# Embedding lookups, pairwise products and a small MLP on one core: a looped program against an unrolled one with a gather ring

## The reference, cut to what matters

```python
e = jnp.stack([tbl_0[ids[:, 0]], ..., tbl_25[ids[:, 25]]], axis=1)
combined = jnp.concatenate([dense_features[:, None, :], e], axis=1)
interactions = jnp.einsum('bfd,bgd->bfg', combined, combined)
z = jnp.concatenate([dense_features, interactions[:, _TRIU_I, _TRIU_J]], axis=1)
h = jnp.concatenate([z, r_dense_features], axis=1)      # 607 columns
h = jnp.maximum(h @ W_top1 + b_top1, 0.0)               # 512
h = jnp.maximum(h @ W_top2 + b_top2, 0.0)               # 256
y = h @ W_top3                                          # 1
```

## Time and profile before

| | |
|---|---|
| device time, median of 3 | 491.5 us (488.62 to 497.02) |
| profiled execution: span | 791.1 us |
| TensorE matmuls busy | 487.2 us, 3016 records |
| VectorE busy | 226.9 us |
| ScalarE busy | 262.0 us |
| GpSimd busy | 305.1 us, of it 304.3 us in 320 gathers |
| mean granted TensorE clock | 0.756 of full speed |

### The profile page before, as it was taken

The page is one execution under the profiler, slowest core; times in us unless marked ns, Lnnn a source line. Parts: engine busy times, 40 slices in busy tenths (PEclk is TensorE's granted clock), DMA queues, the critical chain, the costliest instruction groups (busy, mean ns, idle before and its releaser), DMA issues.

```text
span 791.1 us, 8476 instructions
## 1 busy us (share of the span) xinstructions
PE 487.2 (62%) x3016; PEld 424.6 (54%) x3016; DVE 226.9 (29%) x296; ACT 262.0 (33%) x632; POOL 305.1 (39%) x327
## 2 busy tenths in 40 slices
PE   6407566526748086580956719476393855939977
PEld 4306556426637085470855518464282745827866
DVE  3207251222313142321413213133131332313231
ACT  1115131512416033160522615025150432405762
POOL 6751707370442606336072541705327071350000
PEclk8757767666959679596886959768596866958997
DMA  5620202110110101111010110101101020010000
GB/s 128 198 72 11 54 7 55 28 52 9 34 37 19 53 1 45 27 24 46 0 50 20 35 35 9 52 10 40 30 17 50 3 53 17 27 43 1 1 1 0
DMA packets 20003, 27.57 MB, mean 35 GB/s; under 512 B 10940, under 2 KB 13508, under 8 KB 19985
## 3 DMA queue, kind: packets, MB, share of 16 engines
q0 software_dynamic: 10240, 20.99, 10.3%
q1 hardware_dynamic: 9728, 6.32, 2.9%
q10 hardware_dynamic: 16, 0.01, 0.0%
HBM read 27.29 MB, written 0.01 MB: 35 GB/s over the span
## 4 chain that ended last, share of the span: by engine, by line
PE 42%; another core or an unknown queue 22%; issue 20%; ACT 12%; DVE 3%; DMA 0%; ACTq 0%; SPq 0%; DVEq 0%
PE gram L415 16%; PE ring L453 12%; PE ring L372 11%; ACT xt L585 6%; ACT pairs_or_h L606 4%; DVE onehot L705 2%; PE idb L361 1%; PE ring L442 1%; PE ring L476 1%; ACT xt L574 1%; ACT A L592 1%; DMA pairs_t_or_h<-in_ids 0%; DVE A L786 0%; DVE x_or_h_split L772 0%
## 5 line engine op out<-in xcount | busy, mean ns | idle before, releaser
L321 POOL DMA_INDIRECT rows<-in_tbl,ids_tile x320 | 304.3, 951 | 401.6 <-PE ring L400 306.7
L415 PE MATMUL gram<-xt 128*128 128x104 f32 x1024 | 161.4, 318 | 31.6 <-issue 28.3
L415 PEld LDWEIGHTS gram<-xt 128*128 128x128 f32 x1024 | 153.1, 233 | 38.5 <-issue 33.6
L372 PE MATMUL ring<-onehot,table_hi 125*128 125x256 f32 x368 | 113.1, 334 | 37.6 <-DVE onehot L705 31.3
L705 DVE TENSOR_TENSOR onehot<-idb,vrow 125x2048 fp32r<-125x2048 f32 x48 | 110.0, 2292 | 59.8 <-remote 47.2
L453 PE MATMUL ring<-x_or_h_split,w_hi 128*128 128x256 f32 (+1 forms) x384 | 95.6, 322 | 47.9 <-issue 40.2
L785 DVE COPY A<-gram 32x208 f32<-32x208 f32 x64 | 32.2, 503 | 309.6 <-remote 171.3
L591 ACT COPY A<-gram 32x208 f32<-32x208 f32 x64 | 32.4, 506 | 244.4 <-remote 163.9
L453 PEld LDWEIGHTS ring<-x_or_h_split,w_hi 128*128 128x128 f32 (+1 forms) x384 | 74.1, 219 | 64.0 <-issue 56.8
L372 PEld LDWEIGHTS ring<-onehot,table_hi 125*128 125x128 f32 x368 | 79.9, 217 | 48.0 <-issue 40.2
L372 PE MATMUL ring<-onehot,table_lo 125*128 125x256 f32 x368 | 103.7, 308 | 1.4 <-issue 1.4
(11 more groups left out here) (46 smaller groups left out, 272.9 us busy)
## 6 DMA issues: line engine op xcount, KB each, us to landing
rows<-in_tbl,ids_tile POOLq DMA_INDIRECT x320
xt<-in_tbl SPq DMA_DIRECT2D x6, 500.0 KB
rows<-in_r_dense_features SPq DMA_DIRECT2D x16, 64.0 KB
A<-in_W_top SPq DMA_DIRECT2D x2, 256.0 KB
xt<-in_W_top SPq DMA_DIRECT2D x2, 256.0 KB
pairs_or_h<-in_W_top SPq DMA_DIRECT2D x1, 512.0 KB
ids_tile<-in_ids SPq DMA_DIRECT2D x16, 13.0 KB
pairs_t_or_h<-in_ids SPq DMA_DIRECT2D x1, 208.0 KB
```

Source lines behind the costliest of these rows:

```text
L321: pool.indirect_dma_start(rows[:, t % 2, 1 + r, :], None, aps[f"tbl_{f}"], bass.IndirectOffsetOnAxis(ap=ids_tile[:, t, f:f + 1].bitcast(U3 ...
L372: last = pe.matmul(ps[:, 0:HALF], part[:, m, k, :], onehot[:, buf, k, :], start=(k == 0 and part is table_hi), stop=(k == KT - 1 and part ...
L415: last = pe.matmul(gram[:, s % 2, g // PER_BANK, col:col + QUAD * NA], four, cols, start=True, stop=True)
```

## The change

- The hardware loop is gone; `stages()` yields every stage of four rounds of 512 samples, and all waits are on constants.
- Eight tables instead of six are looked up by one-hot (15 and 19 are added), so 18 are gathered: 288 gathers instead of 320.
- A lookup covers 512 samples, 16 matmuls of 512 columns; its one-hot comes in four quarters (`CH = 4`) of 125 x 1024 through three slots. The ids are spread by a DMA that broadcasts a row of the transposed ids (`spread_ids` on SyncE) and a ScalarE copy into PSUM.
- `rows` is a ring of 45 single rows, not two places of a tile. A gather waits for the transposes of what lay in its slot, and **the first of each six gathers waits until all six of the group ahead have landed**.
- Layers 1 and 2 are plain float32 matmuls of 256 columns, 4 for each block of 128 outputs, without upper and lower parts of weights and activations.
- Of each product step VectorE copies three blocks, ScalarE one; half of the picking of pairs for the first half of a round goes to VectorE.
- All ids are loaded at once, and the eight table loads are split into 112 and 13 partitions. The rows of W_top1 are put in another order on the host so that the one-hot features come last.

```diff
-LOOKUP_TABLES = [2, 5, 10, 12, 13, 14]
+LOOKUP_TABLES = [2, 5, 10, 12, 13, 14, 15, 19]
+ROWS = 45
+GROUP = 6
...
         def _(pool):
-            def gathers(r, t):
-                pool.wait_ge(ids_slot[t], 16 * (r + t // 2 + 1))
-                pool.sem_inc(tiles_begun, 1)
-                for r, f in enumerate(GATHER_TABLES):
-                    pool.indirect_dma_start(
-                        rows[:, t % 2, 1 + r, :], None, aps[f"tbl_{f}"],
-                        bass.IndirectOffsetOnAxis(ap=ids_tile[:, t, f:f + 1].bitcast(U32), axis=0),
-                    ).then_inc(rows_landed[t % 2], 16)
+            def gathers(k):
+                for g, f in enumerate(GATHER_TABLES):
+                    i = k * NG + g
+                    if i >= ROWS and (g == 0 or group_of(i - ROWS) != group_of(i - ROWS - 1)):
+                        pool.wait_ge(ring_filled, filled("rows", *group_of(i - ROWS)))
+                    if i and i % GROUP == 0:
+                        q, u = divmod(i // GROUP - 1, NG // GROUP)
+                        pool.wait_ge(rows_landed[q % 3][u], 16 * GROUP * (q // 3 + 1))
+                    pool.indirect_dma_start(
+                        rows[:, i % ROWS, :], None, aps[f"tbl_{f}"],
+                        bass.IndirectOffsetOnAxis(ap=ids_all[:, k, f:f + 1].bitcast(U32), axis=0),
+                    ).then_inc(rows_landed[k % 3][g // GROUP], 16)
...
         def _(pe):
+                for c in range(CH):
+                    pe.wait_ge(onehot_ready, CH * u + c + 1)
+                    for k in range(KC):
+                        for part in (table_hi, table_lo):
+                            last = pe.matmul(ps, part[:, m, c * KC + k, :], onehot[:, (CH * u + c) % SLOTS, k, :],
...
-                terms = [(k, rows, wp, xp) for k, rows in blocks for wp, xp in ((0, 0), (1, 0), (0, 1))]
+                pe.matmul(ps, w1[:, 0, n * P:(n + 1) * P], x_dense[:, h, :], start=True, stop=False)
+                for k, (k0, w) in enumerate(K_PAIR):
+                    last = pe.matmul(ps, w1[0:w, 1 + k, n * P:(n + 1) * P], x[0:w, k, :], start=False, stop=(k == KX - 1))
...
         def _(dve):
                 dve.tensor_copy(*product_views(t, s, 0))
+                dve.tensor_copy(*product_views(t, s, 1))
+                dve.tensor_copy(*product_views(t, s, 2)).then_inc(gram_dve, 1)
```

More of the change, by code:

```diff
@@ L137, in ring_start @@
[L137 to L157, removed]
+    WARM_UP = 16
@@ L186, in build @@
         b2 = sb("b2", [P, H2 // P])
[L188 to L193, removed]
@@ L364, in lookup @@
-            def lookup(start, buf, m, ready, col):
-                ps = claim(start)
-                pe.wait_ge(onehot_ready, ready)
-                for k in range(KT):
-                    for part in (table_hi, table_lo):
-                        last = pe.matmul(ps[:, 0:HALF], part[:, m, k, :], onehot[:, buf, k, :],
-                                         start=(k == 0 and part is table_hi), stop=(k == KT - 1 and part is table_lo))
-                    if k == 0 and m + 1 < NL:
-                        spread_ids(m + 1, col)
-                last.then_inc(looked_up, 1)
@@ L408, in products @@
+                last.then_inc(ring_filled, 1)
+            def products(r, t, s):
+                n = step_index(r, t, s)
+                if s == 0:
+                    wait_emptied("rows", r, t, NX - 1)
+                if n >= 2:
                     pe.wait_ge(gram_act, n - 1)
@@ L465, in layer2 @@
-            def layer2(H, start, n):
-                ready = [(h1_lo, H1 // P * (H - 1) + k + 1) for k in range(H1 // P)]
-                w = [part[:, :, n * P:(n + 1) * P] for part in w2]
-                split_products(claim(start)[:, 0:HALF], [(k, P) for k in range(H1 // P)], w, h1_split,
-                               ready if n == 0 else None)
-            def layer3(start, after):
-                pe.wait_ge(emptied, after)
-                ps = claim(start)
+                last.then_inc(ring_filled, 1)
@@ new lines, in layer2, with layer3 @@
+            def layer2(r, h, n):
+                if n == 0:
+                    wait_emptied("layer1", r, h, H1 // P - 1)
+                ps = claim("layer2", r, h, n)
+                for k in range(H1 // P):
+                    last = pe.matmul(ps[:, 0:HALF], w2[:, k, n * P:(n + 1) * P], h1[:, k, :], start=(k == 0),
+                                     stop=(k == H1 // P - 1))
+                last.then_inc(ring_filled, 1)
+            def layer3(r, h):
+                wait_emptied("layer2", r, h, H2 // P - 1)
+                ps = claim("layer3", r, h, 0)
```

907 lines of the change are left out of this document (427 added, 480 removed).

## The result

The changed kernel took 520.4 us (median of 5, 519.3 to 526.1) against 491.5 us: a ratio of 1.061, 95% interval 1.055 to 1.067. No change had been forecast, 490 us; it is 6% slower, 30 us over the forecast and inside its range.

The account below looks back on a forecast made before the run. The prediction took gathers and TensorE to tie, the start favouring gathers as bound: last group landed at 443 us, plus 41 for the end and 6 for tied chains, gave 490 us, no change from 491.5; 8-in-10 range 464 to 528.

Parts of the forecast that it names:

- What bounds the changed kernel: GpSimd's gathers and TensorE in a round: 110 us against 109, a tie, with the start favouring the gathers as bound.
- TensorE's path: TensorE's work in a round of 512 samples: 101 us of parts plus an allowance of 8, together 109 us.
- the price of a boundary: GpSimd's wait at every sixth gather: 1.65 us beyond the usual pause, 48 times, 79 us.
- the landing is long: Slower rival at the group wait: a boundary costs up to 3.24 us, kernel 567 us; decides above 1.89; chance 0.17.
- The gathers without boundaries: GpSimd's queue of 288 gathers at 1.25 us each, starting at 4.2 us and needing until 364.2 us.
- Behind the last landing: End of the kernel after the last gather has landed: transposes, product steps, pairs, layers and store, 41 us.
- chains that tie: Whole kernel: the equal gather and TensorE chains hold each other up now and then, 6 us added.
- hand-overs: TensorE's round: 17 us lost between engines before, allowed as 8 us a round after the change.
- the landing is short: Faster rival at the group wait: a boundary costs near 0.94 us, TensorE binds, 475 or 465 us; chance 0.20.
- the rival's own sum: Slower rival on TensorE's round: old surplus stays, 118 to 120 us a round, 505 us in all; chance 0.12.
- the standstills: Kernel before: unexplained stops of 18 to 20 us in each of 16 tiles, about 300 us, taken as hardly in timed runs.
- the standstills are in the timed runs too: Rival on the unexplained stops: the group wait removes them, yet the gather chain stays the floor, time as forecast; no separate chance.

Follow-up runs that it names:

- five of six: Changed kernel, but each group's sixth gather has its own semaphore and the next group waits only for the other five: 467.0 us beside 488.9 for the kernel before.
- four of six: Changed kernel with each group's last two gathers outside the next group's wait: 454.5 us beside 488.9 for the kernel before; in another set 649.1 beside 785.5.

## Why the prediction was wrong

**What bounds the changed kernel: right.** GpSimd pauses at each sixth gather and hardly anywhere else, for longer than TensorE's path needs; a gather is still 1.25 us; taking the wait off gives 455.8 us, so TensorE's path was not the bound. The gathers need 9.5 us for six, 114 us a round, against 97 of TensorE's.

**The step that failed is the price of a boundary.** I took 1.65 us and measured 2.02. The load of ids had given 2.01 from its issue to GpSimd's next gather; I moved down from it towards the store of 1.24 us. That was the wrong neighbour: the store has no GpSimd behind it that must start again, the load has. The prediction took a boundary to be the landing alone, less the 0.30. The landing came 1.55 us after the instruction's end, which makes 1.25, less than the 1.65 taken; what was left out are the 0.77 us from the landing to GpSimd's next gather, and with them it is 2.02. That the load gave 2.01 is in part luck, since it is another kind of DMA, issued by another engine.

So the rival "the landing is long" came in. Its condition was a boundary over 1.89 us, and at 2.3 its sum gave 521 us; measured were 2.02 at most boundaries, 2.31 on the average, and 520.4. Its reason, a group that drains as slowly as a stream of twenty (3.24), is not what the trace shows.

Of the two readings of the Trainium skill (DMA: Bandwidth & Descriptors, "Anatomy of one DMA — SWDGE (gpsimd) path") the one that counts the 2.15 us from the gather's end gave the better price, 1.85 a boundary against 0.9. For the landing itself the other one is nearer: it came 2.50 us after the gather's start. The page's figure ends at the landing, and the 0.77 us behind it are in neither. The measured 2.02 decides.

**The sum, term by term.** The first gather began at 4.5 (forecast 4.2). The gathers without boundaries took 361.3 us (360). The boundaries took 108.6 us and the last landing 1.6, 110 against 79: 47 x 2.02 = 95, and 14 more where a pause was longer. Of these 14 some 6 come from the first seven boundaries, where the table loads run beside the gathers (DMA share 0.88 in the first 20 us): the first pause is 7.5 us, the second 3.7 and the sixth 3.9, while the others there are 1.7 to 1.9. The rest are seven later pauses of 3.0 to 3.9 us, whose cause is not known. None of it was in the sum. Behind the last landing lay 48.3 us against 41. The windows show why:

```profile
476.00:490.00 14.00, 13.55 (x63) 11.32 (x64) 4.11 (x14) 4.39 (x8) 0.00 (x0) 0.55 0.00 1
490.00:524.00 34.00, 29.71 (x159) 24.02 (x157) 6.11 (x21) 11.29 (x31) 0.00 (x0) 0.99 0.00 1
```

TensorE had waited for the last gathers (busy for 7.2 of the 13 us from 463 on, at a granted clock of 0.74), and worked its next 14 us at 0.55, nearly all of it at the lower level, 1.2 GHz: two product steps took 3.67 us each instead of 1.77. With the other pieces there that is about 6 us of the 7 that were missing. The 6 us for chains that tie were not needed, since they don't tie. 4.5 + 361.3 + 108.6 + 1.6 + 48.3 is the span of 524.3. Against the forecast: 17 us for the price of a boundary, 14 for the longer pauses, 7 behind the last landing and 2 elsewhere, less the 6.

**TensorE's path was overrated.** The forecast had 109 us a round, of which 8 were hand-overs, and 475 in all. On a 490 chip without the wait it took 97 a round (the ring stops GpSimd at 172.5, 270 and 367) and the kernel 455.8. In a round there, from 178 to 275 us, TensorE is busy for 95.3 of 97 us, so the hand-overs cost 2 us and not 8. The matmuls themselves are some 5 us under the 101 of the forecast, most of it transposes: four take 0.44 us, 0.11 each, where 0.155 was taken from the earlier trace rows. VectorE's compares are hidden, as said. The rival "the landing is short" put TensorE's path at 465 to 475 us, which is high as well, and its condition, 0.94 us a boundary, was not met; five of six, with about 0.8, took 467.

**Smaller slips.** By the earlier trace rows a half takes 95.5 us and not 96.5; 14 records in 3.29 us are 0.47 us a matmul and not 0.44 (the changed kernel's take 0.43); and by the rival's own sum TensorE's path decides above 118 us a round, not 116. None of them changes the outcome. No run shows the 6 us for chains that tie; they were a guess.

**The two times.** The prediction took the standstills for a mark of the profiled execution, because the medians were 300 us shorter. The number fitted, the cause didn't: by all that the runs show it was another chip. The rival that said the standstills are in the timed runs too, and that the group wait lets the others through, is right on a 790 chip. There the change is a gain of about a third, but the wait is not all of it: in one set the kernel before took 785.5 us, the changed one without the wait 650.1 and with it 521.6, so 135 us come from the rest of the change and 128 from the wait. The trace on which all was read could not tell this; the device time of the same execution beside its span would have.

**What stays open.** What makes the two kinds of chip differ; what TensorE's instructions wait for while they trickle; and why VectorE and ScalarE go on up to 15 us after what they wait for was computed. The runs show only when: in full behind 10 us or so of gathers without a pause, in part within bursts of 7.5 us, and until the gathers end. Even spacing at 1.6 us a gather and five of six were not measured on a 790 chip, so whether it is the pause or the rate is open too. The changed kernel was not timed on a chip known to be a 490 chip. By what was measured it is the best one on a 790 chip, and four of six (454.5 us) the best on a 490 chip.

## What to carry to other kernels

A wait for one's own DMA cost the landing (1.55 us after the instruction's end) and the restart of the issuing engine (0.77) here; read such a price from a row where that same engine waits for a DMA, not from a DMA that nobody restarts behind. Before a limit on what is under way is judged, leave the last one or two transfers out of the wait: where the limit helps nobody, as on a 490 chip, nearly all of its price goes away (454.5 against 520.4 us), and where its pauses or the lower rate help, as on a 790 chip, the gain goes with them (649.1 against 521.6). Where engines wait for something that a profile can't name, look whether the work they need has already ended; here it had, 15 us before. And where a trace and the medians differ by more than their spread, first run the old kernel again beside the new one.

## What the runs showed of the hardware that was not expected

The same program took 489 or 796 us depending on the chip. On two chips a stream of gathers, one in 1.25 us, went with TensorE instructions only every 0.7 us or more, and with copies that began up to 15 us after their product step had ended, although the DMA engines were busy for 0.17 of the time; on two other chips the same stream did nothing. With a pause of 2.3 us after every 7.5 us of gathers the time showed nothing of it (520.9 us on a 790 chip, as in the recorded runs), though copies still came 4 us late; with groups of nine it did (569.6). A gather of 128 rows landed 2.5 us after its start, and GpSimd took 0.77 us from the landing to the next gather.
